# Moving a mixture kernel's side work between the half-tile slots of its engines, and its weight scales into one step

## The reference

```python
q, k = (x @ Wq.T).astype(bf16), (x @ Wk.T).astype(bf16)      # then rope on both
o = sum_over_keys(where(causal, exp(q @ k.T / 16), 0))
x = layernorm(x + relu(o @ fc1_w.T + fc1_b) @ fc2_w.T + fc2_b)
C1, C2, C3 = (softmax_of_top3((x @ P_w.T) @ U.T) for U in (U1, U2, U3))
h = gelu(sum_e C1[:, e] * (x @ W1[e].T))                     # first mixture
y = sum_e C2[:, e] * (h @ W2[e].T) + C3 @ b2                 # second mixture
x = layernorm(x + y)
```

## Time and profile before

| | us |
|---|---|
| median of three runs | 354.75 |
| the profiled execution's own time | 356.04 |
| span of its trace | 354.3 |
| PE busy | 296.2 (84%) |
| DVE busy | 263.5 (74%) |
| ACT busy | 151.8 (43%) |
| GpSimd (POOL) busy | 112.1 (32%) |
| mean granted TensorE clock | 0.949 of full |

### The profile page before, as it was taken

How to read it: one execution, slowest core, us unless ns; L and a number is a source line. 1 busy time by engine, 2 the same in 40 slices (tenths; PEclk the granted TensorE clock), 3 DMA queues, 4 the chain that set the end, 5 groups by cost and what they waited for, 6 DMA issues and landing times.

```text
span 354.3 us, 6374 instructions
## 1 busy us (share of the span) xinstructions
PE 296.2 (84%) x1979; PEld 197.4 (56%) x1981; DVE 263.5 (74%) x884; ACT 151.8 (43%) x321; POOL 112.1 (32%) x264
## 2 busy tenths in 40 slices
PE   0995949689878597899988988988988987998982
PEld 0442424334333364687757757757756756777771
DVE  0169997638955445587997997997997997997782
ACT  1142414544454404624464464464454464443331
POOL 1000396695183300112143143143142143124221
PEclk9999878888988969899999999999999999999998
DMA  8999951990000000000100100100100100101111
GB/s 233 409 400 175 199 91 40 153 104 2 0 1 1 0 2 0 2 0 18 29 18 18 28 18 16 32 17 16 31 16 19 31 16 16 32 17 30 32 31 32
DMA packets 19235, 20.58 MB, mean 58 GB/s; under 512 B 1600, under 2 KB 18432, under 8 KB 18688
## 3 DMA queue, kind: packets, MB, share of 16 engines
q1 hardware_dynamic: 18480, 19.22, 23.2%
q10 hardware_dynamic: 720, 0.93, 0.9%
HBM read 15.94 MB, written 4.19 MB: 57 GB/s over the span
## 4 chain that ended last, share of the span: by engine, by line
DVE 41%; PE 41%; ACT 6%; issue 6%; POOL 2%; DMA 2%; ACTq 0%; DVEq 0%; POOLq 0%
PE bank L776 20%; DVE early L1106 13%; PE bank L642 10%; DVE amaxp L918 4%; PE bank L689 3%; DVE idx L1006 3%; DVE stats L977 3%; DVE st L1125 2%; DVE early L1130 2%; PE bank L655 2%; DVE xsin L903 2%; DMA gatew<-in_gate 2%; PE bank L741 1%; DVE xcos L902 1%; ACT x1T L528 1%
## 5 line engine op out<-in xcount | busy, mean ns | idle before, releaser
L776 PE MATMUL bank<-W,early 128*128 (+1 forms) x630 | 75.5, 273 | 4.4 <-DVE early L1106 2.9
L776 PE MATMUL bank<-W,x1T 128*128 (+1 forms) x630 | 78.7, 281 | 0.3 <-DVE early L1106 0.3
L642 PE MATMUL bank<-early,wqk 128*128 128x512 f32 x128 | 70.9, 692 | 8.8 <-DMA gatew<-in_gate 8.8
L776 PEld LDWEIGHTS bank<-W,x1T 128*128 128x128 f16 x630 | 61.3, 101 | 21.3 <-DVE early L1106 9.3
L776 PEld LDWEIGHTS bank<-W,early 128*128 128x128 f16 x630 | 59.8, 98 | 14.4 <-issue 4.3
L1106 DVE SCALAR_TENSOR_TENSOR early<-bank,Csel,early 128x256 f32<-128x256 f32 x124 | 59.3, 478 | 8.9 <-PE bank L776 5.5
L439 POOL TENSOR_SCALAR ve<-mv 128x1 f32<-128x1 f32 x32 | 7.2, 226 | 122.1 <-DVE mv L1126 122.1
L642 PEld LDWEIGHTS bank<-early,wqk 128*128 128x128 f32 x128 | 26.1, 221 | 34.0 <-issue 24.2
L481 ACT ACTIVATE qk<-bank 128x512 bf16<-128x512 f32 x32 | 19.0, 594 | 51.3 <-PE bank L642 51.3
L564 ACT ACTIVATE early<-early 128x256 f32<-128x256 f32 x32 | 13.3, 417 | 53.5 <-DVE early L1106 53.4
L902 DVE TENSOR_TENSOR xcos<-qk,cb 128x1024 bf16<-128x1024 bf16 x16 | 11.0, 686 | 26.2 <-ACT qk L481 26.1
(11 more groups left out here) (103 smaller groups left out, 446.4 us busy)
## 6 DMA issues: line engine op xcount, KB each, us to landing
early<-in_xT SPq DMA_DIRECT2D x16, 256.0 KB, 8.3
xs<-in_x SPq DMA_DIRECT2D x32, 128.0 KB, 7.6
out<-early SPq DMA_DIRECT2D x32, 128.0 KB
W<-in_w1T SPq DMA_DIRECT2D x1, 2048.0 KB, 12.1
W<-in_w2T SPq DMA_DIRECT2D x1, 2048.0 KB, 12.3
W<-in_w1T SPq DMA_DIRECT2D x1, 1024.0 KB, 7.7
W<-in_w2T SPq DMA_DIRECT2D x1, 1024.0 KB, 13.8
wqk<-in_wqkT ACTq DMA_DIRECT2D x1, 512.0 KB, 4.1
```

Source lines behind the costliest of these rows:

```text
L642: mm = pe.matmul(bank[PROJ[n % 2]][:, :], wqk[:, k, g, :], xTb[:, c % 4, k, :, :].rearrange("p s n -> p (s n)"), start=(k == 0), stop=(k = ...
L776: mm = pe.matmul(where[:, 0:DIM], lhs(hx, c), w, start=(k == 0), stop=(k == 5))
```

## The change

- The side work is placed anew in the `aux` of PE, ACT, DVE and POOL. PE's side work now stands mostly in position 0 of a tile (between X and Y), DVE's mostly in position 1 (between hlo and the adds of X). `EARLY` has one slot more in front, so everything in the chunks comes a quarter of a chunk later.
- The scales come in one step: PE's two peak steps in chunk 3, DVE's `peak_pow` in chunk 3 and `scales` with `router_split` in chunk 4. Weight splitting moves to chunks 4 to 7, on GpSimd four pieces to a chunk.
- W2's scale rests on sums of absolute values, three ScalarE instructions over 2048 columns each (`w_sum`), and DVE only takes their maximum (`w_bound`); the three reductions of W2 are gone. The constant 256 becomes `TOP` = 16384.
- The scaled copy of the logits moves from DVE (`route_max`) to ACT (`z_copy`).
- Tile 1's first mixture stands ahead of the transposes of tile 0's h, on PE, ACT and DVE.

`ones2`, `peak` and `diag` grow to three rows, `peak_transpose`, `peak_spread`, `peak_pow` and `scales` lose their argument and work on all three columns at once, and `w_piece`, `w_high` and `route_logits` wait for `scale_done` 1. The rest of the diff, cut to its core:

```diff
-        EARLY = [(-3, 3, 1)] + [(k, s, pos) for k in (-2, -1) for s in range(GT) for pos in range(2)]
+        EARLY = [(-3, 3, 0), (-3, 3, 1)] + [(k, s, pos) for k in (-2, -1) for s in range(GT) for pos in range(2)]
...
             def aux(k, s, pos):
-                if (s, pos) == (1, 1) and group(k + 2):
+                if (s, pos) == (0, 1) and group(k + 2):
                     norm_scale(k + 2)
-                if (s, pos) == (2, 1) and group(k + 1):
+                if (s, pos) == (3, 0) and group(k + 1):
                     chosen_exps(k + 1)
                 if (s, pos) == (3, 1) and group(k + 1):
                     weights_of(k + 1)
...
                     early_aux(c, j, aux)
-                    if c >= 2 and j and piece < NM * (NE - NB):
+                    if c >= 4:
                         w_piece(piece)
                         piece += 1
...
+            def w_sum(q):
+                act.wait_ge(ld_w[1], 32)
+                act.activation(junk[:, :, :], Wf[:, WS:2 * WS, :][:, PARTS[q], :], ACT.Abs,
+                               accum_out=amaxp[:, 1, q:q + 1]).then_inc(asum_done, 1)
+                if q < 2:
+                    act.wait_ge(asum_done, q + 1)
...
+            def z_copy(g):
+                act.wait_ge(z_done, g + 1)
+                wait(act, mask_done, g)
+                act.activation(zs[:, :, :].rearrange("p g e -> p (g e)"), bank[MISC][:, 0:Z], ACT.Copy,
+                               scale=iscale[:, 0:1]).then_inc(z_copied, 1)
...
             def aux(k, s, pos):
                 if (s, pos) == (0, 0):
+                    if group(k):
+                        C3T_copy(k)
                     if group(k + 1):
                         x1_high(k + 1, 1)
-                    if group(k):
-                        C3T_copy(k)
                 if (s, pos) == (1, 0) and group(k + 1):
-                    exp_route(k + 1)
-                if (s, pos) == (2, 0) and group(k + 2):
+                    z_copy(k + 1)
+                if (s, pos) == (1, 1) and group(k + 2):
                     normed(k + 2, 0)
-                if (s, pos) == (2, 1) and group(k + 2):
-                    normed(k + 2, 1)
+                if (s, pos) == (2, 0):
+                    if group(k + 1):
+                        exp_route(k + 1)
+                    if group(k + 2):
+                        normed(k + 2, 1)
...
-                if 3 <= c <= 6:
-                    w_high(2 * (c - 3))
+                if c == 2:
+                    w_sum(1)
+                if c >= 4:
+                    w_high(2 * (c - 4))
                 qk_copy(c, 2)
...
+                if c in (1, 2):
+                    w_sum(2 * (c - 1))
+                if c >= 4:
+                    w_high(2 * (c - 4) + 1)
...
             for i in range(1, NT + 2):
                 k, s = divmod(i, GT)
                 aux(k, s, 0)
+                if i == 1:
+                    begin(1)
...
             def aux(k, s, pos):
-                if (s, pos) == (0, 0) and group(k):
-                    C3_transpose(k)
-                if (s, pos) == (0, 1):
+                if (s, pos) == (0, 0):
+                    if group(k):
+                        C3_transpose(k)
+                    if group(k + 2):
+                        fc(k + 2, 1)
+                    if group(k + 1):
+                        x1_transpose(k + 1, 1)
+                if (s, pos) == (1, 0):
                     if group(k + 1):
                         route_logits(k + 1)
-                    if group(k + 2):
-                        fc(k + 2, 1)
-                if (s, pos) == (1, 1) and group(k):
-                    bias(k, 0)
-                if (s, pos) == (2, 1):
                     if group(k):
-                        bias(k, 1)
-                    if group(k + 2):
-                        x1_transpose(k + 2, 0)
-                if (s, pos) == (3, 0) and group(k + 1):
+                        bias(k, 0)
+                if (s, pos) == (2, 0) and group(k):
+                    bias(k, 1)
+                if (s, pos) == (2, 1) and group(k + 2):
+                    x1_transpose(k + 2, 0)
+                if (s, pos) == (3, 0) and group(k + 3):
+                    fc(k + 3, 0)
+                if (s, pos) == (3, 1) and group(k + 1):
                     route_count(k + 1)
-                if (s, pos) == (3, 1):
-                    if group(k + 2):
-                        x1_transpose(k + 2, 1)
-                    if group(k + 3):
-                        fc(k + 3, 0)
...
-                if c in (2, 3):
-                    peak_transpose(c - 2)
+                if c == 3:
+                    peak_transpose()
...
-                if c in (2, 3):
-                    peak_spread(c - 2)
                 early_aux(c, 2, aux)
                 if c:
                     scores(c - 1, 1)
                 project(c, 3)
+                if c == 3:
+                    peak_spread()
...
-            first(range(0, NE // 2))
+            first(range(0, 4))
             scores(NCH - 1, 0)
-            first(range(NE // 2, NE))
+            first(range(4, 7))
             scores(NCH - 1, 1)
+            first(range(7, NE))
...
                 k, s = divmod(i, GT)
                 aux(k, s, 0)
+                if i == 1:
+                    load_ids(0)
+                    mixture(1, 0, lambda hx, c: x1T[:, 1, hx, c, :], range(TOPK))
...
+            def w_bound():
+                dve.wait_ge(asum_done, 3)
+                dve.tensor_reduce(amax[:, 2:3], amaxp[:, 1, :], AX.X, ALU.max).then_inc(amax_done, 1)
...
-                dve.wait_ge(z_done, g + 1)
-                link(dve.tensor_scalar(zs[:, :, :].rearrange("p g e -> p (g e)"), bank[MISC][:, 0:Z], iscale[:, 0:1], None,
-                                       ALU.mult))
+                dve.wait_ge(z_copied, g + 1)
...
             def aux(k, s, pos):
-                if (s, pos) == (0, 0):
+                if (s, pos) == (0, 1):
                     if group(k + 2):
-                        fc_add(k + 2, 0)
+                        fc_add(k + 2, 1)
+                        norm_stats(k + 2)
                     if group(k + 1):
                         x1_low(k + 1, 1)
-                if (s, pos) == (0, 1) and group(k + 1):
-                    route_max(k + 1)
-                if (s, pos) == (1, 0):
-                    if group(k + 2):
-                        fc_add(k + 2, 1)
-                    if group(k + 1):
-                        route_index(k + 1, 0)
-                if (s, pos) == (1, 1) and group(k + 2):
-                    norm_stats(k + 2)
-                if (s, pos) == (2, 0):
+                if (s, pos) == (1, 1):
                     if group(k):
                         bias_add(k, 0)
                     if group(k + 1):
-                        route_index(k + 1, 1)
-                if (s, pos) == (2, 1) and group(k + 1):
-                    route_mask(k + 1)
-                if (s, pos) == (3, 0):
+                        route_max(k + 1)
+                if (s, pos) == (2, 0) and group(k + 1):
+                    route_index(k + 1, 0)
+                if (s, pos) == (2, 1):
                     if group(k):
                         bias_add(k, 1)
+                    if group(k + 1):
+                        route_index(k + 1, 1)
+                if (s, pos) == (3, 0) and group(k + 1):
+                    route_mask(k + 1)
+                if (s, pos) == (3, 1):
+                    if group(k + 3):
+                        fc_add(k + 3, 0)
                     if group(k + 2):
                         x1_low(k + 2, 0)
-                if (s, pos) == (3, 1) and group(k + 1):
-                    route_sums(k + 1)
+                    if group(k + 1):
+                        route_sums(k + 1)
             dve.wait_ge(ld_const, 16 * 6)
             for c in range(NCH):
                 early_aux(c, 0, aux)
                 early_aux(c, 1, aux)
-                if c in (2, 3):
-                    peak_pow(c - 2)
+                if c == 4:
+                    scales()
+                    router_split()
                 rope(c, 0)
                 if c == 0:
                     router_matrix()
-                if c in (1, 2):
-                    w_amax(c - 1, 0)
-                if c in (2, 3):
-                    scales(c - 2)
-                    if c == 2:
-                        router_split()
                 if c == 1:
-                    w_amax(0, 1)
+                    w_amax(0)
+                if c == 3:
+                    peak_pow()
                 early_aux(c, 2, aux)
-                if 3 <= c <= 6:
-                    w_low(2 * (c - 3))
+                if c >= 4:
+                    w_low(2 * (c - 4))
                 early_aux(c, 3, aux)
                 rope(c, 1)
+                if c == 1:
+                    w_amax(1)
                 if c == 2:
-                    w_amax(1, 1)
-                if c in (1, 2):
```

(86 more changed lines are left out.)

48 lines of the change are left out of this document (14 added, 34 removed).

## The result

The changed kernel takes 369.76 us, the median of four runs (368.95 to 371.6), beside 354.86 us for the kernel before on the same chip: a ratio of 1.0428 (1.0396 to 1.0461), slower by 14.9 us. The profiled execution took 368.95 us, its span is 367.0 us, and the mean granted clock 0.935 of full where it was 0.949. Two of the four runs of experiment e10 fell in a slower state and are compared with nothing.

The account below looks back on a forecast made before the run. PE and DVE were taken as nearly full in the main loop, DVE as the chain in the chunks. Start -20, groups 1 to 5 +25, group 6 +1.5 make +6.5 on 356.04: 362.5, median 361, range 347 to 371 us.

Parts of the forecast that it names:

- The walk: Main-loop group traced through PE, DVE and ACT: PE waits of 2.25 us (logits), 1.25 (fc) and 2.9 (C3 transpose).
- walked period: Main-loop group at full clock with the new placement: 29.9 us instead of 26.5.
- clock term: Main loop: PE's clock falls after the two long waits, costing 1.6 us a group together, ends 0 and 3.3.
- step 1: Group from C3 transpose through X: PE through at 6.05 us, DVE's x1_low at 8.2, logits wait 2.25 us.
- The start: Chunks up to tile 0's Y: begins about 127.7 instead of 147.75 us, winning 20; up to 10 more without contention.
- Group 6: Main-loop group without norm_stats: its waits cost some 1.5 us more than before.
- the tail: Group 7, which has only biases: change of 0.
- B: Rival, main loop: same waits but the clock stays up, -1.8 us in all, so 353 us; chance 0.20.
- C: Rival, chunks: POOL slows DVE less, rope halves at 2.1 us, start -30; 351 us, or 343 without clock loss; chance 0.18.
- D: Rival: two half-clock stretches a group fully on the path (3.3 us) and full contention, +19, so 374 us; chance 0.07.
- E: Rival, main loop: waits vanish and a group takes DVE's 24.1 us, so 323 us; chance 0.03.

Follow-up runs that it names:

- e10: The kernel of e2 with eight more unread matmuls ahead of fc in groups 1 to 4; 357.53 and 359.94 us in the two comparable runs.
- e1: The changed kernel with two DVE slots reordered, x1_low and route_sums put first in theirs; 342.15 us, ratio 0.9651.
- e5: The changed kernel with old aux, old EARLY and logits copy on DVE, keeping one scale step, ACT's sums and tile 1's early mixture; 344.44 us.
- e7: The kernel of e3 with tile 1's first mixture back behind the transposes of tile 0's h; 331.09 us, ratio 0.9325.
- e4: The kernel before with only the new aux and EARLY; two scale steps, W2's peaks and logits copy on DVE, tile 1 in its old place; 384.89 us.
- e2: The changed kernel with 14 unread matmuls ahead of the C3 transpose and of the logits in groups 1 to 6; 357.41 us, ratio 1.0075.
- e3: The changed kernel with the old placement in all engines from group 0 on, the logits' copy staying on ACT; 329.87 us, ratio 0.9311.

## Why the prediction was right or wrong

**Right: the kind of loss and its places.** The walk gave waits of 2.9, 2.25 and 1.25 us; measured are 2.74, 2.54 and 1.33, released by POOL's C, by `x1_low` and by `bias_add`, as it said. The third is called "issue" in the trace, and `bias_add` is read from the times. The walked period at full clock was 29.9 us; e10's group at full clock, which has these producers and filler in the waits, takes 30.4. The walk missed only small steps, such as the 0.20 us ahead of the second bias. e1 shows the cause of two of the three waits: with the producers first, the one for the logits goes and the one for C3 falls to 1.54.

**Wrong: the size of the clock term.** The step that failed is the sentence that took 1.6 us a group for both waits together. In the group shown each of the two waits costs a whole mixture at half speed, 3.79 - 2.14 and 3.81 - 2.14, together 3.3 us, which is the upper end that I gave. Against e10's groups at full clock (30.43 us, and 29.83 for group 5, which has no `fc` to wait for) the five groups are longer by 4.6, 3.3, 1.3, 3.3 and 3.3 us, a mean of 3.2: in group 1 the clock was low already ahead of the mixture (`fc` took 2.07 us), and group 3 has one slow mixture only. My reason for half of it was that part of the slow stretch would fall on X, which has slack in step 1. It mostly doesn't: the slow stretch falls on Y, and DVE, which has worked off everything while PE waited, stands idle for it (2.36 us), so hlo and all that follows move by the full amount. X ran at 2.13 again. The groups came out at 33.5 us on average instead of 31.5: +34.7 instead of +25.0. About 7.8 us of the difference of 9.7 is the clock term (15.8 for the five groups where I had 8.0) and about 2 the walked period.

**The start.** It gained 25.2 us where I took 20 (10 more was the bound). The parts of my sum stood well, each a little high: scales at 50 for 49.2, W2's sums 1.89 us each for 2, and rope halves from start to start of 3.87, 3.77, 3.81, 3.07, 3.77, 2.8, 2.2 and 2.1, a mean of 3.2 for 3.4. `L934` in chunk 4 took 1.65 us, as in the earlier trace rows. The `w_low` beside it took 1.53, but the eight of them took 0.75 to 1.53 and 8.2 us together, where I had 10.0. The last two halves took no more than undisturbed ones: POOL's pieces of weight splitting pause from 94.0 to 101.2 us, where POOL first waits 2.16 us for DVE and then does routing work.

DVE came to tile 0's first adds at 104.7, where I had 109.6; from there to its second mixture it took 17.8 us for 18.1. What my walk did not tell apart is where the gain is from: e5 shows 11.65 us for the one scale step and the sums on ACT, with some 0.8 of it from tile 1's early mixture by e7, and e4 shows 12.83 for the placement in the chunks alone, which e4's expectation had put at under 5.

**Group 6** cost 2.0 us for 1.5, and the tail 0.2 for 0. By these terms the sum is -24.3 + 34.7 + 2.0 + 0.2; the two errors in the large terms, -4.3 and +9.7, have opposite signs. The rest of the way from +6.5 to +14.9 is that the profiled execution of before was above its median and that of the changed kernel below. 369.76 us lies in the range near its upper end, and slower was the likeliest verdict, but that the time lies inside the range is partly luck: with the start as I had it, it would have been 374.

**The rivals.** B, in which the clock stays up, is excluded: two stretches of 3.4 us at half speed in 33.75 make a mean clock of 0.90, which is what the windows row has. e2 shows the least that B would have been worth, since it has the late producers but not the low clock behind the first two waits: 12.4 us less than the changed kernel. The 15.8 us above would give 354, close to B's 353. B was the case of the Trainium skill, page "TensorE: Matmul & The Clock Gate", section "HAM oscillation — how this bites in real kernels", which lets the clock fall only for gaps longer than any of these; the trace disagrees, at 2.54 and 2.74 us, and the runs with filler do at 1.33 (e2) and at 1.01, 1.20 and 1.21 (e10). C (rope halves under 2.6 us) was half right for the last chunks. D had the clock term right with 3.3 and the start wrong; its loop, +33, is the nearest to the measured one. E is excluded by groups of 33.5 us. A better order does exist, though not E's 24.1 us a group: e3 has 26.1 and a start as early as the changed kernel's.

**Open.** In e10 the same wait of 1.2 us was followed by both levels of the clock, and in e2 the wait of 1.33 us by a slow mixture that the changed kernel doesn't have there. In e1 1.30 us ahead of the C3 transpose of group 1 was followed by 3.52 us, and 1.54 in groups 2, 3 and 5 by full speed. Nor does a long wait alone do it: 2.42 us in group 6 did not, with 0.6 us of small matmuls between it and the mixture instead of 1.8 or more in the other groups. What decides was not found, and no run here varied one wait, or the small work behind it, by itself.

## What to carry to other kernels

When side work is written into slots between two engines, put the producer that the other engine meets next first in its slot and what only fills time last: here the order inside two slots was worth 27.6 us of 370. Cost a wait like those of 2.5 us here as the wait plus the next mixture at half clock (1.7 us more), until a run shows that the clock stays up: in groups 1 to 5 of the changed kernel and of e4 it was so behind 19 of 20 such waits. And time the parts of a mixed change separately: this one held a start 24 us better and a loop 37 us worse, and keeping the first without the second gives a kernel 7% faster than the one before, though the whole change made it 4% slower.

## What the runs showed of the hardware

Adding work to TensorE made the kernel faster: 168 matmuls that nobody reads took it from 369.8 to 357.4 us, with the producers as late as before, and the granted clock of a group at 0.94 instead of 0.90. And the half-clock stretch is not tied to the longest wait. With two waits filled, a third of 1.33 us was followed by a mixture of 3.26 us instead of 2.14, and filling that one as well brought slow mixtures of 3.47 and 3.81 us back at waits of 1.20 and 1.01 us. The same wait need not give the same clock, so a fill at some of the waits of a group is to be judged by all of its mixtures, not by the one behind it.
